# The tail of two chained cross attentions: another order of the take-out, the last heads, the exponentials and the hi copies

## What is computed

```
normed = x * rsqrt(mean(x*x) + 1e-6) * norm_w
q, k, v = split_heads(normed @ wq), split_heads(ctx @ wk), split_heads(ctx @ wv)
attn = softmax(einsum('bhqd,bhkd->bhqk', q, k), axis=-1)
x1 = x + merge_heads(einsum('bhqk,bhkd->bhqd', attn, v)) @ wo
w = softmax(einsum('brd,bfd->brf', x1, ctx), axis=-1)
out = x1 + einsum('brf,bfd->brd', w, ctx)
```

## Time and profile before

| what | value |
|---|---|
| median of 3 runs | 699.72 us (698.96 to 700.08) |
| the profiled execution | 699.38 us |
| its span | 697.6 us |
| TensorE busy | 675.7 us (97%) |
| VectorE busy | 465.6 us (67%) |
| ScalarE busy | 467.8 us (67%) |
| GpSimd busy | 160.7 us (23%) |
| granted TensorE clock, mean | 0.995 |

### The profile page before, as it was taken

How to read it: one execution, slowest core, us unless ns; L and a number is a source line. 1 busy time by engine, 2 the same in 40 slices (tenths; PEclk the granted TensorE clock), 3 DMA queues, 4 the chain that set the end, 5 groups by cost and what they waited for, 6 DMA issues and landing times. The chain is left out here.

```text
span 697.6 us, 13322 instructions
## 1 busy us (share of the span) xinstructions
PE 675.7 (97%) x4764; PEld 613.6 (88%) x4764; DVE 465.6 (67%) x994; ACT 467.8 (67%) x1169; POOL 160.7 (23%) x485
## 2 busy tenths in 40 slices
PE   5899999999999999999999999999999999999986
PEld 4688989998999889999899889999899888999885
DVE  3586666777567875677666775677766776577733
ACT  4767676677666766667766776667766777666742
POOL 2211133111322114111142114211142212422110
PEclk9999999999999999999999999999999999999997
DMA  6012112111021002220121111202013011112000
GB/s 188 1 54 16 8 12 53 16 8 9 15 55 15 16 1 23 53 16 8 16 51 11 16 9 15 55 14 16 1 15 60 9 16 15 9 9 16 9 12 7
DMA packets 25566, 16.50 MB, mean 24 GB/s; under 512 B 14334, under 2 KB 23838, under 8 KB 25502
## 3 DMA queue, kind: packets, MB, share of 16 engines
q1 hardware_dynamic: 25502, 15.66, 14.7%
HBM read 15.19 MB, written 0.46 MB: 22 GB/s over the span
## 5 line engine op out<-in xcount | busy, mean ns | idle before, releaser
L546 ACT ACTIVATE pT<-ps_t 128x496 fp32r<-128x496 f32 (+1 forms) x312 | 182.4, 587 | 179.8 <-PE ps_t L940 177.6
L697 DVE TENSOR_REDUCE part_max<-ps_s 124x1 f32<-124x512 f32 (+2 forms) x336 | 209.5, 651 | 60.1 <-PE ps_s L916 59.0
L964 PE MATMUL ps_o<-pT,c_both 128*128 128x248 f32 (+2 forms) x1632 | 242.9, 291 | 0.6 <-DVE result L748 0.5
L683 DVE TENSOR_TENSOR pT<-ps_t,pT 128x496 fp32r<-128x496 f32 (+3 forms) x312 | 192.0, 623 | 69.5 <-ACT pT L546 67.7
L964 PEld LDWEIGHTS ps_o<-pT,c_both 128*128 128x128 f32 x1632 | 219.4, 189 | 3.6 <-DVE pT L683 2.6
L555 ACT ACTIVATE probs<-ps_s,neg_max 124x512 f32<-124x512 f32 (+2 forms) x336 | 219.1, 663 | 1.4 <-DVE neg_max L702 1.4
L940 PE MATMUL ps_t<-ident,probs 124*128 124x124 f32 (+2 forms) x1232 | 184.1, 268 | 5.1 <-DVE pT L683 1.9
L940 PEld LDWEIGHTS ps_t<-ident,probs 124*128 124x128 f32 (+2 forms) x1232 | 146.1, 140 | 44.8 <-ACT probs L555 10.1
L429 POOL CAST tails<-probs 124x36 fp32r<-124x36 f32 (+2 forms) x224 | 40.6, 213 | 489.7 <-ACT probs L555 489.7
L912 PE MATMUL ps_s<-cT_hi,q_hi 128*124 128x512 f32 (+3 forms) x312 | 143.5, 460 | 1.2 <-DVE q_lo L683 1.2
L916 PE MATMUL ps_s<-cT_hi,q_lo 128*124 128x512 f32 (+3 forms) x312 | 118.8, 381 | 0.0
(11 more groups left out here) (130 smaller groups left out, 492.8 us busy)
## 6 DMA issues: line engine op xcount, KB each, us to landing
ctx_raw<-in_ctx_dram SPq DMA_DIRECT2D x8, 704.0 KB
rinv_row<-denominator_rows SPq DMA_DIRECT2D x39, 124.0 KB, 3.7
rinv_row<-denominator_rows SPq DMA_DIRECT2D x8, 186.0 KB, 3.5
denominator_rows<-rinv SPq DMA_DIRECT2D x39, 1.0 KB
wq_sb<-in_L_xattn_wq_dram SPq DMA_DIRECT2D x2, 256.0 KB, 6.1
wk_sb<-in_L_xattn_wk_dram SPq DMA_DIRECT2D x2, 256.0 KB, 6.3
wv_sb<-in_L_xattn_wv_dram SPq DMA_DIRECT2D x1, 512.0 KB, 7.8
wo_sb<-in_L_xattn_wo_dram SPq DMA_DIRECT2D x1, 512.0 KB, 8.9
```

The lines of the kernel that those rows point to most:

```text
L546: act.activation(dst, ps_t[:, turn_bank("item", g, c), 0:nj * m] .rearrange("p (j m) -> p j m", m=m), ACT.Copy).then_inc(turned_hi, 1)
L683: dve.tensor_tensor(dst, src, hi.bitcast(F32), ALU.subtract).then_inc(done, 1)
L697: mx = dve.tensor_reduce(part_max[0:m, k, c:c + 1], ps_s[0:m, score_bank(g, c), 0:CHUNKS[c][1]], AX.X, ALU.max)
L964: t = pe.matmul(ps_o[:, 0, 0:w], weights, moving, start=(i == 0), stop=(i == UNITS - 1))
```

## The change

Nothing is changed in the arithmetic but for the last batch's result. On VectorE the take-out, x1_T and x1_lo move ahead of L_FIRST's three lo parts; the result of B-2 moves behind L_LAST's first lo part. On TensorE heads 13 to 15 move ahead of L_FIRST's turns, and the third of these turns moves between L_LAST's first and second chunk of scores. On ScalarE x1_hi moves behind L_FIRST's first hi copy; two of L_LAST's exponentials move ahead of the scaled copy of B-2, and its first hi copy ahead of the third exponential; x1_rows moves to the end. The scaled copy of B-1 and the add go, and a multiply-add on VectorE takes their place, which reads ps_o's second half itself.

```
@@ ScalarE
             exp_chunk(L_FIRST, 2)
-            for c in range(NC):
-                turned_chunk_hi(L_FIRST, c)
+            turned_chunk_hi(L_FIRST, 0)
             act.wait_ge(x1_ready, B)
             act.activation(x1_hi[:, :], x1_T[:, :], ACT.Copy).then_inc(x1_hi_done, 1)
+            turned_chunk_hi(L_FIRST, 1)
+            turned_chunk_hi(L_FIRST, 2)
+            exp_chunk(L_LAST, 0)
+            exp_chunk(L_LAST, 1)
             late_scaled(B - 2)
-            for c in range(NC):
-                exp_chunk(L_LAST, c)
+            turned_chunk_hi(L_LAST, 0)
+            exp_chunk(L_LAST, 2)
+            turned_chunk_hi(L_LAST, 1)
+            turned_chunk_hi(L_LAST, 2)
             act.wait_ge(x1_turned, B)
             act.activation(x1_rows[(B - 1) % 2][0:Q, :], ps_m[0:Q, 0, 0:D], ACT.Copy).then_inc(x1_rows_ready, 1)
-            for c in range(NC):
-                turned_chunk_hi(L_LAST, c)
-            late_scaled(B - 1)
@@ VectorE
             turned_chunk_lo(T_LAST, 2)
-            turned_chunk_lo(L_FIRST, 0)
-            turned_chunk_lo(L_FIRST, 1)
             take_out_last()
             x1_made(B - 1)
             dve.wait_ge(x1_hi_done, B)
             lo_part(x1_lo[:, :], x1_T[:, :], x1_hi[:, :], x1_split)
-            turned_chunk_lo(L_FIRST, 2)
+            for c in range(NC):
+                turned_chunk_lo(L_FIRST, c)
             invert_late(L_FIRST)
             for c in range(NC):
                 chunk_maximum(L_LAST, c)
+            turned_chunk_lo(L_LAST, 0)
             late_result(B - 2)
-            for c in range(NC):
-                turned_chunk_lo(L_LAST, c)
+            turned_chunk_lo(L_LAST, 1)
+            turned_chunk_lo(L_LAST, 2)
             invert_late(L_LAST)
-            dve.wait_ge(late_lo_out, B)
+            dve.wait_ge(pv_done, block(B - 1, LATE))
+            dve.wait_ge(late_inverted, B)
             dve.wait_ge(x1_rows_ready, B)
-            dve.tensor_tensor(late_sum[0:Q, :], late_lo[0:Q, :], x1_rows[(B - 1) % 2][0:Q, :], ALU.add)\
+            dve.scalar_tensor_tensor(out=late_sum[0:Q, :], in0=ps_o[0:Q, 0, D:2 * D],
+                                     scalar=rinv[0:Q, stat(L_LAST):stat(L_LAST) + 1],
+                                     in1=x1_rows[(B - 1) % 2][0:Q, :], op0=ALU.mult, op1=ALU.add)\
                 .then_inc(late_added, 1)
             late_result(B - 1)
@@ TensorE
             project(last, range(9, 13))
+            wait_heads(last, range(13, 16))
+            project(last, range(13, 16))
             turn(L_FIRST, 0)
             turn(L_FIRST, 1)
-            wait_heads(last, range(13, 16))
-            project(last, range(13, 16))
+            pe.wait_ge(row_copied, 1)
+            scores(L_LAST, 0)
             turn(L_FIRST, 2)
-            for c in range(NC):
-                if c == 0:
-                    pe.wait_ge(row_copied, 1)
-                scores(L_LAST, c)
+            scores(L_LAST, 1)
+            scores(L_LAST, 2)
```

## The result

The changed kernel takes 693.46 us (median of 4 runs, 692.71 to 693.79), the kernel before 699.85 us (median of 4, 698.96 to 700.08). The ratio is 0.9911, with a 95% interval of 0.9898 to 0.9925. In the profiled execution the span went from 697.6 to 691.7 us.

The account below looks back on a forecast made before the run. The tail was taken as one dependency chain with three queue-order waits, under a falling clock. Gains of 2.55, 1.65, 0.21 and 0.33 us summed to 4.74, giving 694.7 us for the profiled execution and a 695.0 us median; range 693.3 to 696.8.

Parts of the forecast that it names:

- third part: End of the tail: a scaled copy and an add after the last product, counted as queue waiting, result written 695.26 to 695.61.
- Take-out, heads, x_T, first scores: Tail's start: take-out right behind its product, heads 13 to 15 2.50 us earlier, L_LAST's first scores 2.55 us earlier.
- Turn between the scores: L_FIRST's third turn on TensorE, placed between L_LAST's score chunks, costs no wait and stands at 678.7.
- Exponentials: ScalarE: L_LAST's first exponential at 682.5, 4.2 us earlier, 2.3 from earlier scores and 1.9 from the order.
- Tail columns: Before the last product: GpSimd's split ends last, putting the last transposition at 686.08, 4.41 us earlier.
- Two multiply-adds: VectorE at the end: product end to result end takes 0.78 us instead of 1.11, a gain of 0.33 us.
- Last product: TensorE, last transposition to product end: the same 4.01 us as before, mostly at half clock, ending at 690.09.
- Rival 1: The last product stays at 2.4 GHz, 1.4 us less: 693.6 us, chance 0.15.
- rivals 2 and 3: L_LAST's scores still at 1.2 GHz, 696.4 us, chance 0.17; low clock from heads to end, 699.7 us, chance 0.04.
- rival 4: TensorE waits for the take-out with nothing in its queue and the low clock lasts: 702.4 us, chance 0.03.
- a missed wait: One of the new orders brings another queue wait, worth 1 to 2 us: 696.5 us, chance 0.06.
- Rival 2: L_LAST's scores still run at 1.2 GHz, third exponential held to 685.95: 1.4 us lost, 696.4 us, chance 0.17.

Follow-up runs that it names:

- delay run: Changed kernel plus two unread copies on ScalarE between L_LAST's maximum and its first exponential: 695.47 us, ratio 0.9944 to the kernel before.
- filled kernel: Kernel before, order unchanged, with all four TensorE holes in the tail filled with unread identity transpositions: 696.53 us, ratio 0.9957 to the kernel before.

## Why the prediction was right, and where it was off

*What bounds the kernel.* Right in the main. The tail was one chain with two waits on queue order, and both went. The third part that the prediction names, the scaled copy and the add at the end, was no such wait: the scaled copy started at 694.53, 0.03 us behind the product. The take-out and the heads came within 0.1 us of where they were put, and so did every step up to the last transposition within 0.16 us.

*Take-out, heads, x_T, first scores.* Right: 2.90 us behind the landmark, 2.94 forecast. The wait of x_hi for a hi copy was rightly seen, 0.40 us from 677.40 to 677.80. Its price was not: the run with x_hi first gained 0.23 us from 0.44.

*Turn between the scores.* The forecast held it for free and gave no worth to it. The run without it was 2.70 us slower in the tail, 1.21 by VectorE's wait and 1.48 in the last product, at 0.60.

*Exponentials.* Right: the first one 7.44 us behind the landmark, 7.53 forecast; the scaled copy of B-2 didn't wait, since its product ended at 683.25 and it started at 684.10.

*Tail columns.* Right: the split became what ends last before the final transposition, as the row with [0.21 <-POOL tails L431] says.

*Two multiply-adds.* Right: 0.78 us, both in the changed kernel and (0.77) alone.

*Last product.* This term was mis-sized. It was put at 4.01 us, with half clock as before; it took 2.66 us at 1.00. The step that failed is the sentence that the idle time ahead of it is "of the same kind as before". It was 2.9 us with TensorE busy for 1.57. The 3.7 us with 1.18 before end ahead of the last turn; from the end of B-2's product to the last transposition, 686.4 to 690.5, it is 4.10 us with 1.58:

```profile
686.40:690.50 4.10, 1.58 (x13) 1.22 (x13) 1.41 (x3) 3.25 (x10) 1.07 (x4) 0.96 0.05 12
```

So TensorE did the same work there in both kernels, in 1.2 us less time after the change. The delay run made it 4.0 us again with 1.57, and the product was at 0.58; with the 4.0 us filled it was back at 1.00. The forecast weighed the kind of the stretch, not its length.

*The range.* Rival 1 had this outcome and its time, 693.6, at a chance of 0.15. The measured 693.46 us lies only 0.16 above the lower end of the range, and it lies in it because the range takes in rival 1; the sum alone, 695.0, missed by 1.5 us. To that extent the hit is luck.

*The other rivals.* None came. Scores at 1.00 speak against rivals 2 and 3, a take-out 0.20 us behind the landmark against rival 4, and steps that all fell within 0.16 us against a missed wait. Rival 2's sum has a slip: with the durations it uses, the third exponential would stand at 684.93 + 0.27 + 0.45 = 685.65 and not at 685.95, which makes its time 696.1. The range and the forecast don't rest on it.

*Attribution.* The sum put 2.55 us to the order up to the scores and 1.65 us to the exponentials. The filled kernel shows that 2.88 of the 6.25 us can be had with the old order, by keeping TensorE busy. In the sum the clock's part in the scores was booked as order, though rival 2 had priced it, at 1.4 us; the filled kernel's first exponential came 1.33 us earlier by it.

*Open.* Where a fall comes is not settled by the length of a gap alone: the kernel with the two multiply-adds alone had the kernel before's gaps and full clock in the scores, and the kernel with the third turn behind the scores lost it behind 3.1 us in which TensorE was busy for 1.63. For the changed kernel, that all four of its runs have a mean clock of 0.999 or 1.000 is what is shown, not that no run could have less.

## What to carry to other kernels

In a tail that is one chain, read for each wait whether data or the queue ends it, and move the instruction whose data is there; rebuilding the timetable from starts and durations of rows gave six steps in a row within 0.2 us. Cost TensorE's work behind a sparse stretch at both clock levels, and look at how long the stretch will be after the change: here a shorter one gave back 1.35 us besides the waits. Filling the holes with useless transpositions is a cheap way to find out what the clock costs, and here, on the old order, a gain of 0.4% by itself.

## What the runs showed of the hardware

- A product of 23 matmuls took 2.6 to 2.7 us, from the last transposition ahead of it, at granted clock 1.00, and 4.0 to 4.7 us at 0.61 to 0.50 (0.61 is the kernel before from 690.5 to 694.5). The slow ones stood behind stretches, from the end of the product before to that transposition, in which TensorE was busy for 1.5 to 1.7 of 3.1 to 4.2 us.
- With TensorE busy for 1.57 of 2.90 us ahead of it, 1.43 of 2.30, or 3.55 of 4.00, it kept 1.00. These are one execution each, the two groups lie close (1.63 of 3.10 fell, 1.57 of 2.90 did not), and no limit between them was measured.
- The same gaps brought the fall at another place in another kernel's execution (scores at 1.00, all of the last product at 0.50).
- A multiply-add on VectorE that reads 100 x 128 from PSUM takes 0.35 us, and the next one that needs its result starts 0.03 to 0.04 us behind it.
